# Attention totals kept in one PSUM bank, and exponents read from PSUM, in a graph network kernel

## What is computed

```
h = (x @ W.T).reshape(n, 8, 32)
alpha = sum(h[src] * a_src) + sum(h[dst] * a_dst)            # per edge and head
enc = relu(edge_attr @ edge_W.T + edge_b)
alpha = leaky_relu(alpha + sum(enc * h[dst]), 0.2)
ex = exp(alpha - segment_max(alpha, dst)[dst])
out = segment_sum(h[src] * ex, dst) / max(segment_sum(ex, dst), 1e-10) + bias
```

## Time and profile before

| | us |
|---|---|
| three timed runs | 2416.58, 2420.48, 2431.32 |
| their median | 2420.48 |
| span of the profiled execution, first to last instruction | 2421.0 |
| VectorE / TensorE busy in the span | 1638.0 / 1785.6 |
| GpSimd / ScalarE busy in the span | 1152.8 / 805.9 |
| attention: first VectorE instruction to last copy of totals | 1408.6 to 2074.7 |

### The profile page before, as it was taken

How to read it: one execution, slowest core, us unless ns; L and a number is a source line. 1 busy time by engine, 2 the same in 40 slices (tenths; PEclk the granted TensorE clock), 3 DMA queues, 4 the chain that set the end, 5 groups by cost and what they waited for, 6 DMA issues and landing times. The chain is left out here.

```text
span 2421.0 us, 41392 instructions
## 1 busy us (share of the span) xinstructions
PE 1785.6 (74%) x11452; PEld 1386.4 (57%) x11452; DVE 1638.0 (68%) x3379; ACT 805.9 (33%) x2077; POOL 1152.8 (48%) x1106
## 2 busy tenths in 40 slices
PE   3466666655179996399992878888887887499598
PEld 1245445544057775299991546666665665255587
DVE  8655565555167778655556849999999999764443
ACT  7433333322000002333331644444444444244221
POOL 0277777777700000055550057777777776000243
PEclk9677887887589999599996889999999999799799
DMA  3355555544388862522225145555555553533353
GB/s 86 110 190 192 188 189 173 172 167 165 128 298 284 294 216 103 200 64 73 71 68 180 39 146 146 145 150 142 151 152 145 145 144 113 194 131 119 123 180 104
DMA packets 203758, 368.03 MB, mean 152 GB/s; under 512 B 63193, under 2 KB 111162, under 8 KB 203159
## 3 DMA queue, kind: packets, MB, share of 16 engines
q1 hardware_dynamic: 148066, 205.99, 26.2%
q0 software_dynamic: 54624, 159.35, 21.3%
q10 hardware_dynamic: 850, 0.04, 0.0%
HBM read 235.32 MB, written 130.87 MB: 151 GB/s over the span
## 5 line engine op out<-in xcount | busy, mean ns | idle before, releaser
L2136 POOL DMA_INDIRECT att_rows<-hdram,top_ix x440 | 502.8, 1143 | 264.0 <-issue 133.8
L874 POOL DMA_INDIRECT mtab<-first_w,msgs_ix x280 | 277.5, 991 | 85.3 <-issue 81.1
L1177 POOL IOTA route_spare<- 128x65 f32 (+1 forms) x2 | 0.4, 177 | 522.3 <-POOLq L1115 522.3
L2217 PE MATMUL att_p_acc<-att_msg,att_hot 128*128 128x264 f32 x880 | 225.8, 401 | 14.7 <-DVE wts_wn L2396 6.5
L736 PE MATMUL msgs_p_m<-nodes_n,msgs_hott 128*128 x592 | 185.1, 467 | 48.8 <-issue 30.7
L2251 ACT ACTIVATE att_enc<-att_p_z 128x1024 f32<-128x1024 f32 x110 | 112.7, 1024 | 308.8 <-PE att_p_z L2157 308.8
L2217 PEld LDWEIGHTS att_p_acc<-att_msg,att_hot 128*128 128x128 f32 x880 | 163.4, 196 | 53.2 <-issue 26.6
L874 POOL DMA_INDIRECT mtab<-msgs_rw,msgs_ix x160 | 160.6, 1004 | 68.9 <-issue 44.8
L2166 PE MATMUL att_p_h<-heads_parts,att_hz 128*128 x1320 | 184.3, 295 | 1.4 <-DVE att_enc L2323 1.4
L637 DVE TENSOR_TENSOR first_w<-msgs_p_m,msgs_sorted 128x1024 f32<-128x1024 f32 x70 | 85.6, 1223 | 140.3 <-PE msgs_p_m L736 113.1
L736 PEld LDWEIGHTS msgs_p_m<-nodes_n,msgs_hott 128*128 128x128 f32 x592 | 132.4, 235 | 76.7 <-issue 56.0
(11 more groups left out here) (408 smaller groups left out, 3811.7 us busy)
## 6 DMA issues: line engine op xcount, KB each, us to landing
first_w<-mtab SPq DMA_DIRECT2D x77, 520.0 KB, 4.6
etab<-msgs_et SPq DMA_DIRECT2D x110, 288.0 KB, 2.5
att_hz<-etab SPq DMA_DIRECT2D x110, 288.0 KB, 2.9
msgs_rw<-mtab SPq DMA_DIRECT2D x45, 520.0 KB, 4.7
htab<-hid_hr SPq DMA_DIRECT2D x12, 1024.0 KB, 4.3
first_w<-in_L_ffn_w SPq DMA_DIRECT2D x16, 512.0 KB, 5.0
ffn0x_w<-in_L_ffn_w SPq DMA_DIRECT2D x16, 512.0 KB
ffn_w<-in_L_ffn_Wd SPq DMA_DIRECT2D x8, 1024.0 KB
```

What stands on the lines that cost most here:

```text
L874: nc.gpsimd.indirect_dma_start(mtab, bass.IndirectOffsetOnAxis(ap=ix[:, g, q:q + 1], axis=0), rw[g % RS][:, q, :], None).then_inc(s_free[g ...
L2136: nc.gpsimd.indirect_dma_start(rows[:, g % RS, q, :], None, hdram, bass.IndirectOffsetOnAxis(ap=ix1[:, g, q:q + 1], axis=0)).then_inc(s_ro ...
L2217: last = T.matmul(p_acc[u % 2][:, 0:HW], hot[g % 2][:, q, :], msg[g % 2][:, q, :], start=(r == 0), stop=(r == UQ - 1))
```

## The change

The running totals stay in one PSUM bank, `p_sum`. TensorE adds each unit's sums onto it. ScalarE waits for them, copies the bank into `acc`, and then multiplies the bank in place by `keep` of the next unit (0 or 1); only then TensorE may add the next unit. Where the next unit is the first of a block, VectorE multiplies it in place by `fall` instead (`lessen`). VectorE's `gathered`, the four tiles of totals and the loan are gone.

The bank that this frees holds the exponents of two blocks (`p_ex`). ScalarE takes the exponentials twice: into `ex` in SBUF, from which `weights` still reads, and into `p_ex`, from which VectorE's `messages` reads. ScalarE's second one waits for all messages before the step, and the messages wait for ScalarE's newest write to the bank.

The order in a step changes too. TensorE: sums of the first unit of group s - 8; line or tops; offsets(s); own_tiles, encoders of s + 1; sums of the second unit; destinations(s + 1); turn_back or edge_tops. ScalarE: keep_totals of the first unit of group s - 8; exponents; encodings(s + 1); keep_totals of the second; copy_back or falls; weights and widen of group s - 7. VectorE: lessen; differences; products(s); segments or maxima; messages(s - 7); alphas. The loop has two steps fewer.

```diff
-    total = [a.sb(f"total{s}", [P, HW])[:] for s in two] + [lent[:, 0:HW] for lent in spare]
-    p_acc = [a.ps(f"p_acc{s}", [P, 512]) for s in two]
+    p_sum = a.ps("p_sum", [P, 512])[:, 0:HW]
+    bank = a.ps("p_ex", [P, 512])
+    p_ex = [bank[:, k * BC * H:(k + 1) * BC * H].rearrange("p (c h) -> p c h", h=H) for k in two]
...
+            def sums(u):
+                g, t = u // GU, u // BU
+                if u % GU == 0:
+                    pe.wait_ge(s_msg, g + 1)
+                    pe.wait_ge(s_wide, g + 1)
+                    pe.wait_ge(s_weight, g + 1)
+                if u % BU:
+                    pe.wait_ge(s_same, u - t)
+                elif t:
+                    pe.wait_ge(s_less, t)
+                for r in range(UQ):
+                    q = u % GU * UQ + r
+                    last = T.matmul(p_sum, hot[g % 2][:, q, :], msg[g % 2][:, q, :], start=(u == 0 and r == 0),
+                                    stop=(u == NU - 1 and r == UQ - 1), skip_group_check=True)
+                last.then_inc(s_acc, 1)
...
-            for s in range(NUG + LAG + 3):
-                t, j = s // BG, s % BG
+            for s in range(NUG + LAG + 1):
+                t, j, at = s // BG, s % BG, (s - LAG - 1) * GU
+                if 0 <= at < NU:
+                    sums(at)
                 if j == 0 and 0 < t <= NB:
                     line(t - 1)
...
                     encoders(s + 1)
+                if 0 <= at < NU:
+                    sums(at + 1)
+                if s + 1 < NUG:
                     destinations(s + 1)
...
-                if 0 <= s - LAG - 1 < NUG:
-                    sums(s - LAG - 1)
...
+            def keep_totals(u):
+                b = act.value_load(gb[0:1, u:u + 1], min_val=0, max_val=NT - 1)
+                act.wait_ge(s_acc, u + 1)
+                if u:
+                    act.wait_ge(s_kept, u)
+                S.copy(acc[:, bass.ds(b, 1), :].rearrange("p a c -> p (a c)"), p_sum).then_inc(s_kept, 1)
+                if (u + 1) % BU and u + 1 < NU:
+                    act.wait_ge(s_kept, u + 1)
+                    S.mul(p_sum, p_sum, keep[:, u + 1:u + 2]).then_inc(s_same, 1)
+
+            def exponents(t, done):
...
                 S.activation(ex[t % 2][:, 0:w], al[t % 2][:, 0:w], ACT.Exp).then_inc(s_ex, 1)
+                if done > 0:
+                    act.wait_ge(s_msg, done)
+                S.activation(p_ex[t % 2][:, 0:w], al[t % 2][:, 0:w], ACT.Exp).then_inc(s_pex, 1)
...
-                dve.wait_ge(s_ex, t + 1)
+                dve.wait_ge(s_pex, min(NB, (g + LAG - BG - 2) // BG + 1))
...
-                                bc(ex[t % 2][:, j * G:(j + 1) * G, :], 3, D), ALU.mult).then_inc(s_msg, 1)
+                                bc(p_ex[t % 2][:, j * G:(j + 1) * G, :], 3, D), ALU.mult).then_inc(s_msg, 1)
+            def lessen(t):
+                dve.wait_ge(s_fall, t + 1)
+                dve.wait_ge(s_kept, t * BU)
+                V.tensor_tensor(p_sum.rearrange("p (h d) -> p h d", d=D + 1), p_sum.rearrange("p (h d) -> p h d", d=D + 1),
+                                bc(fall[t % 2][:], 2, D + 1), ALU.mult).then_inc(s_less, 1)
```

More of the change, by code:

```diff
@@ L2064, in split, with attention @@
     link(V.tensor_copy(parts[2], rest))
-def attention(nc, a, cst, etab, segtab, ewz, ix1, penn, gb, keep, hparts, hdram, acc, spare):
-    RS, SE, TS = 12, 10, 4
+def attention(nc, a, cst, etab, segtab, ewz, ix1, penn, gb, keep, hparts, hdram, acc):
+    RS, SE = 12, 10
     two = range(2)
@@ L2099, in attention @@
     (s_z, s_enc, s_h, s_prod, s_red, s_adst, s_al, s_line, s_chain, s_rb, s_back, s_backc, s_top, s_new, s_fall, s_edge,
-     s_dif, s_ex, s_msg, s_wide, s_acc, s_add, s_go, s_weight, s_kept) = (a.sem(m) for m in (
+     s_dif, s_ex, s_msg, s_wide, s_acc, s_same, s_less, s_weight, s_kept, s_pex) = (a.sem(m) for m in (
          "z", "enc", "h", "prod", "red", "adst", "al", "line", "chain", "rb", "back", "backc", "top", "new", "fall", "edge",
-         "dif", "ex", "msg", "wide", "acc", "add", "go", "weight", "kept"))
+         "dif", "ex", "msg", "wide", "acc", "same", "less", "weight", "kept", "pex"))
     s_rows, s_hz, s_seg = ([a.sem(f"{m}{s}") for s in range(k)] for m, k in (("rows", RS), ("hz", SE), ("seg", 2)))
@@ L2288, in exponents @@
                 S.activation(ex[t % 2][:, 0:w], al[t % 2][:, 0:w], ACT.Exp).then_inc(s_ex, 1)
+                if done > 0:
+                    act.wait_ge(s_msg, done)
+                S.activation(p_ex[t % 2][:, 0:w], al[t % 2][:, 0:w], ACT.Exp).then_inc(s_pex, 1)
             encodings(0)
             widen(0)
[L2292 to L2295, removed]
+            for s in range(NUG + LAG + 1):
+                t, j, at = s // BG, s % BG, (s - LAG - 1) * GU
+                if 0 <= at < NU:
+                    keep_totals(at)
+                if j == 2 and 0 < t <= NB:
+                    exponents(t - 1, s - LAG)
                 if s + 1 < NUG:
                     encodings(s + 1)
+                if 0 <= at < NU:
+                    keep_totals(at + 1)
                 if j == 0 and 0 < t <= NB:
@@ L2402, in _ @@
             link(V.memset(turns[:], -2.0 * BIG))
-            link(V.memset(total[TS - 1][:], 0.0))
-            for s in range(NUG + LAG + 3):
-                t, j = s // BG, s % BG
+            for s in range(NUG + LAG + 1):
+                t, j, at = s // BG, s % BG, s - LAG - 1
+                if 0 < at < NUG and at % BG == 0:
+                    lessen(at // BG)
+                if j == 2 and 0 < t <= NB:
+                    differences(t - 1)
                 if s < NUG:
@@ L2411, in _ @@
                     maxima(t - 1)
[L2412 to L2416, removed]
                 if 0 <= s - LAG < NUG:
```

21 lines of the change are left out of this document (1 added, 20 removed).

## The result

The changed kernel takes 2464.07 us (median of four runs, 2461.9 to 2467.01) against 2422.57 of the kernel before (four runs): a ratio of 1.0165, 95% interval 1.0146 to 1.0184. It is slower by 41.5 us. 59 were forecast (2480, range 2415 to 2515).

What follows compares the result with a forecast made beforehand. GpSimd was taken to set the pace, VectorE right behind; a TensorE-ScalarE loop of 25.1 us a block replaces them: 2421.0 + 43.4 (steady stretch) + 15.2 (tail) = 2479.6, say 2480 us, range 2415 to 2515.

Steps and rivals of the forecast that it cites:

- What bounded the kernel before: Steady stretch: GpSimd never waits and sets the pace at 23.4 us a block, with VectorE (94% busy) right behind.
- The exponents part: Exponents read from PSUM free GpSimd's gathers from VectorE's message multiply: a block of gathers falls to 20.1 us.
- The loop: Steady stretch: a round trip between TensorE and ScalarE becomes the limit, 24.74 us a block at the full clock.
- plain step: A step without block-start or block-end work, from TensorE's first sums to the next first sums: 5.70 us.
- the wait on its own copy: ScalarE's gap between copying the totals and scaling the bank: taken 0.17 us, bounds 0.05 and 0.3.
- the scaling: ScalarE's in-place multiply of the PSUM bank: 0.50 us, bounds 0.41 and 0.6.
- the encoders' load: TensorE's weight load for the encoders, counted from its first sums: T + 2.30 us, in a block's second step T + 3.8.
- 3.57 later: Block's second step: time from the release of the tops' wait to the encoders' load, used for T + 3.8 us.
- the sums till ScalarE sees them: TensorE's sums of one unit, 1.0 us long plus 0.2 until seen: 1.2 us in the tail's round trips.
- The clock: Steady stretch: loss from TensorE's halved clock, taken as 0.4 us a block, bounds 0 and 1.5.
- The tail: From the last encoders to the last copy's end: each unit becomes a round trip, 50.4 us together, +15.2 us.
- Rival A: Register loads and ScalarE's tail both hide, so GpSimd's gathers or TensorE's own work limit: 2358 us, chance 0.12.

Runs made afterwards that it cites:

- e7: The kernel before, with TensorE's two register loads of window numbers moved to the start of its step: 2423.49 us, ratio 1.0000.
- e1: The changed kernel with the messages reading exponents from SBUF again and ScalarE's second exponential removed: 2460.21 us, ratio to the kernel before 1.0149.
- e3: The changed kernel with TensorE's two register loads of window numbers moved ahead of the first sums' waits: 2394.22 us, ratio to the kernel before 0.9873.
- e2: The changed kernel with sums, totals and scaling by fall one step later (group s-9 in place of s-8): 2426.99 us, ratio to the kernel before 1.0018.
- e10: The changed kernel with eight useless matmuls where TensorE waits at the end of each block's first step: 2439.84 us, ratio to the kernel before 1.0067.
- e8: The changed kernel with register loads first, TensorE kept busy in the tail, and sums one step later: 2366.58 us, ratio to the kernel before 0.9769.
- e9: e8 with the messages reading the exponents from SBUF: 2403.07 us, ratio to the kernel before 0.9910.
- e6: The changed kernel with register loads first, TensorE kept busy in the tail, and messages reading exponents from SBUF: 2385.36 us, ratio to the kernel before 0.9841.
- e11: The changed kernel without ScalarE's in-place scaling of the bank, TensorE's next sums waiting for the copy alone: 2424.06 us, ratio to the kernel before 0.9997.

## Why the prediction was right or wrong

**What bounded the kernel before** holds. The control e7 confirms that TensorE's gaps were free, and the earlier trace rows give the pace by themselves.

**The exponents part** did what the forecast said: 0.953 us a gather, idle time that is a wait. That this wouldn't be needed was right (e1).

**The loop** was right in kind, in each place named: the register loads behind a wait (e3), ScalarE's widening (e2), the turned maxima ahead of it, the sum of TensorE's own order in the last step. It was too long in size. Forecast at the full clock 5.70 (plain step), 5.24 (last), 6.50 (first) and 7.30 (second); measured 5.4, 4.95, 6.14 and 6.2, 22.7 in place of 24.74. The terms, from the timeline above:

- the wait on its own copy ("bounds 0.05 and 0.3, taken 0.17") is 0.03 us, below my lower bound. I had read it from two copies with a register load between them, which is a row of something else;
- the scaling takes 0.455 us, not 0.50, and the copy out of PSUM 0.378, not 0.41 (that row was a copy out of SBUF);
- the encoders' load comes at +2.21 and not 2.30; in the second step at +3.01 and not 3.8. This is the largest miss: "3.57 later" was counted from the release of the tops' wait, but TensorE was then still busy with the eight sums before them, so 1.54 of the 3.57 was queue. From the first tops matmul to the encoders' load it is 2.03 us before and 2.04 after, and in the new order the tops come 0.97 after the sums;
- the sums till ScalarE sees them were taken at 1.2; the row gives 1.27 (2071.53 to 2072.80), and after it is 1.25, so this term was a little too short;
- TensorE starts 0.06 to 0.10 us after ScalarE's end (0.11 taken).

**The clock** was too small: "I take 0.4 a block". It is about 1.1 (23.85 against 22.7), and e10 gets 0.8 of it back. The row read for it had 1.3 us a block (2.77 against 1.47); taking 0.4 of them supposed that most would be hidden, but the second step lies on the path and nearly all of it counts. Before the clock falls, TensorE has stood idle in two pieces of 1.0 and 1.2 us around the start of a block's second step; with the first of them filled (e10) the clock stayed full in 22 of 25 second steps, in place of 6.

**The tail** was sized for the full clock, and for that it was right: 50.4 forecast, 47.6 with TensorE kept busy. In the changed kernel it takes 61.2, since from 2065 us on the clock is 1.2 GHz throughout. The step that failed is that I gave the clock a price in the steady stretch and none in the tail.

The errors had opposite signs. In the stretch, measured less forecast is -31 us: the loop's size alone gives (22.7 - 24.74) x 25.25 = -52, and the clock gives some 19 back. The tail gives +11. That the total missed by only some 17 us is in part luck: the clock, priced too low twice, made up for a loop priced too long. Rival A's condition ("it needs both hidden") is borne out by e8: with the loads and ScalarE's end off the path the time is 2366.6, against 2358 priced for it, with gathers of 0.955 us. The limit there is the loop at 20.78 us a block and not the gathers' 20.2.

The Trainium skill ("SBUF — State Buffer", Who interferes with whom) has GpSimd's SBUF reads held by a VectorE instruction with two SBUF inputs. The runs agree, 0.953 us with one SBUF input and up to 2.0 with two. The inference of the same section, that descriptor generation isn't held by such a multiply, fails for a gather that starts while the multiply runs (up to 2.0 us); one that has started before it does run on unheld (last section). The queue of 64 instructions that the Trainium skill gives TensorE ("TensorE: Matmul & The Clock Gate", table of specifications) doesn't help behind a wait, as e3 shows by the 70 us that two loads ahead of the wait give.

## What to carry to other kernels

Work taken from the fullest engine is worth only what the next loop allows; write that loop out as a round trip over engines, with the sequencer's register loads and dispatch in it, before moving an accumulator into a single buffer. Where an engine stands at a wait anyway, put its register loads ahead of the wait: the same two loads were worth 0 us in the kernel before and 70 us in this one. Where a change turns a stretch into short round trips of TensorE, as in this tail, price the stretch at 1.2 GHz as well as at 2.4 (61.2 and 47.6 us here), and try added matmuls.

## What the runs showed that was not expected

**When a gather is held.** The gather's mean with both message operands in SBUF was 1.156, 1.034, 1.028 and 1.075 us in four orders of the same instructions. The timeline of e9, message multiplies and gathers:

```profile
1701.65 1.23 DVE L2401 TENSOR_TENSOR att_msg<-att_rows,att_ex 128x1024 f32<-128x1024 f32 x1
...
1701.70 2.00 POOL L2137 DMA_INDIRECT att_rows<-hdram,top_ix  x1 [0.31 <-issue]
...
1706.52 0.95 POOL L2137 DMA_INDIRECT att_rows<-hdram,top_ix  x1 [0.31 <-issue]
1706.67 1.23 DVE L2401 TENSOR_TENSOR att_msg<-att_rows,att_ex 128x1024 f32<-128x1024 f32 x1 [1.22 <-PE att_p_sum L2221]
...
1707.77 0.95 POOL L2137 DMA_INDIRECT att_rows<-hdram,top_ix  x1 [0.30 <-issue]
...
1711.16 1.23 DVE L2401 TENSOR_TENSOR att_msg<-att_rows,att_ex 128x1024 f32<-128x1024 f32 x1 [0.78 <-PE att_p_sum L2221]
...
1711.54 1.67 POOL L2137 DMA_INDIRECT att_rows<-hdram,top_ix  x1 [0.30 <-issue]
```

A gather that starts while the multiply runs ends 0.82 us after the multiply's end (1702.88 to 1703.70; 1712.39 to 1713.21). One that started before it (1706.52) is not held at all. And one that starts near the multiply's end (1707.77, end 1707.90) loses nothing. So which of the two starts first decides: of 291 gathers that started before their multiply, by as little as 0.02 us, none took more than 1.08 us. The loss depends on the phase between the two engines, from 0 to 1.1 us.

The traces bear this out throughout. In the five runs whose messages read both operands from SBUF (before, e1, e6, e7, e9), 468 gathers start while a multiply runs. A rule, "it ends 0.82 us after the multiply, but takes at least 0.95", gives the time of 464 of them within 0.03 us. By where the gathers start it gives means over all 440 of 1.136, 1.036, 1.023, 1.146 and 1.066 us, where 1.143, 1.028, 1.024, 1.151 and 1.068 are measured. So the phase makes the different means. In the kernel before, where GpSimd and VectorE ran in step, 100 of the 110 multiplies met a gather's start. What sets the phase of a run was not tried.

**The clock in the tail.** Through round trips in which TensorE was busy 2.10 of 3.15 us the granted clock stayed at 1.2 GHz for over 40 us. The same trips with added matmuls ran at 2.4.

**A shorter chain can give twice.** In e3 the gaps went and with them the halved clock (0.99 granted). Not so in e11, which has 0.95 there, about as the changed kernel. Why the encoders' load comes sooner in its third step stays open. The 4 us ahead of group 0 need no cause in the edit: the encoders of group 0 start between 1407.2 and 1413.1 us in the profiles of these kernels, whose code up to there is the same. The rest of the 40 us is that of single executions: the profiled one lay 2.2 us below its median in the changed kernel and 2.4 above it in e11.
